# Attention and three residual blocks on one core: four background banks, single score banks, and maximum units in bursts of two

## What is computed

```
x = x + attn(layernorm(x))
    scores = K Q^T / 8;  scores[q < k] = 1e-10
    probs  = softmax(scores);  out = (probs V) W_out + bias
x = x + ffn(layernorm(x))
    w = (q / 7.5 - 1) * scale  (per group of 16);  y = x w^T + bias + (x la^T) lb^T
```

## Time and profile before

| | |
|---|---|
| three timed runs, us | 2410.23, 2406.73, 2414.44 (median 2410.23) |
| profiled execution: time, span | 2404.84, 2403.0 |
| PE busy | 2249.6 us, 94% of the span |
| VectorE, ScalarE, GpSimd busy | 1312.2, 869.7, 1341.8 us |
| mean granted clock of TensorE | 0.981 |

### The profile page before, as it was taken

How to read it: one execution, slowest core, us unless ns; L and a number is a source line. 1 busy time by engine, 2 the same in 40 slices (tenths; PEclk the granted TensorE clock), 3 DMA queues, 4 the chain that set the end, 5 groups by cost and what they waited for, 6 DMA issues and landing times. The chain is left out here.

```text
span 2403.0 us, 30679 instructions
## 1 busy us (share of the span) xinstructions
PE 2249.6 (94%) x10080; PEld 1147.3 (48%) x10080; DVE 1312.2 (55%) x3555; ACT 869.7 (36%) x1266; POOL 1341.8 (56%) x1231
## 2 busy tenths in 40 slices
PE   5999999999999998999999999999999988899987
PEld 2344444444444444444444444444444444767764
DVE  4755555555555555464646463646464663365664
ACT  3244444433434335434343434343434343011111
POOL 2176767666767676676767575757575741111110
PEclk9699999999999999999999999999999999999998
DMA  4534444443535362535353535363635431521100
GB/s 115 131 95 125 113 125 113 116 121 104 134 103 134 99 173 72 139 94 139 91 147 87 148 86 149 79 158 79 156 78 157 107 94 54 188 88 62 62 18 18
DMA packets 206268, 261.30 MB, mean 109 GB/s; under 512 B 74720, under 2 KB 91296, under 8 KB 206112
## 3 DMA queue, kind: packets, MB, share of 16 engines
q1 hardware_dynamic: 206112, 259.35, 40.9%
HBM read 169.87 MB, written 88.87 MB: 108 GB/s over the span
## 5 line engine op out<-in xcount | busy, mean ns | idle before, releaser
L689 POOL TENSOR_TENSOR acc<-acc,probs 128x512 f32<-128x512 f32 (+1 forms) x900 | 970.8, 1115 | 387.7 <-ACT probs L1039 387.7
L1039 ACT ACTIVATE probs<-ps_s 128x1024 f32<-128x1024 f32 (+2 forms) x640 | 551.9, 899 | 414.6 <-PE ps_s L836 172.8
L1094 DVE TENSOR_REDUCE partial<-ps_bg 128x1 f32<-128x512 f32 x768 | 491.1, 685 | 232.7 <-PE ps_bg L778 230.6
L834 PE MATMUL ps_s<-qq,kk 128*128 128x512 f32 (+3 forms) x1280 | 574.5, 449 | 26.8 <-ACT probs L1039 26.8
L855 PE MATMUL ps_o<-probs,v 128*64 128x512 f32 (+3 forms) x2560 | 541.2, 544 | 5.2 <-DVE num L1118 5.1
L836 PE MATMUL ps_s<-qm,kl 128*128 128x512 f32 (+3 forms) x1280 | 469.0, 366 | 0.0
L726 PE MATMUL ps_bg<-home,w_in 128*128 128x512 f32 x768 | 366.5, 601 | 14.9 <-DVE split L1076 10.8
L834 PEld LDWEIGHTS ps_s<-qq,kk 128*128 128x128 f32 x1280 | 244.6, 191 | 213.8 <-issue 155.2
L778 PE MATMUL ps_bg<-k_bf,q_bf 64*128 64x512 bf16 (+3 forms) x1280 | 272.3, 365 | 44.1 <-DVE split L1076 21.1
L1091 DVE CUSTOM_DVE_ANT_0 junk<-ps_bg,mask_q 128x512 bf16<-128x512 f32 (+3 forms) x512 | 230.8, 485 | 103.6 <-issue 102.4
L855 PEld LDWEIGHTS ps_o<-probs,v 128*64 128x64 f32 x2560 | 155.9, 136 | 236.1 <-issue 209.4
(11 more groups left out here) (109 smaller groups left out, 1889.1 us busy)
## 6 DMA issues: line engine op xcount, KB each, us to landing
high_and_low<-split SPq DMA_DIRECT2D x128, 512.0 KB, 5.9
qq<-high_and_low SPq DMA_DIRECT2D x64, 512.0 KB, 4.3
kk<-high_and_low SPq DMA_DIRECT2D x128, 256.0 KB, 5.2
qm<-high_and_low SPq DMA_DIRECT2D x64, 256.0 KB, 5.9
kl<-high_and_low SPq DMA_DIRECT2D x64, 256.0 KB, 6.3
e<-masked_weights SPq DMA_DIRECT2D x128, 128.0 KB, 3.0
scale<-inverse_sums SPq DMA_DIRECT2D x128, 128.0 KB, 2.9
heads_turned<-num SPq DMA_DIRECT2D x64, 256.0 KB, 3.5
```

Source lines behind the costliest of these rows:

```text
L689: g.tensor_tensor(acc[h][:, group % 2, q0:q0 + w], acc[h][:, group % 2, q0:q0 + w], probs[h][:, probs_slot(i, t), at:at + w], ALU.add).the ...
L834: pe.matmul(out, kk[:, h, kb * P:(kb + 1) * P], qq[:, h, q], start=True, stop=False, skip_group_check=True)
L1039: nc.scalar.activation(probs[h][:, probs_slot(i, t), 0:width], ps_s[:, h, 0:width], ACT.Exp, scale=SCORE_SCALE).then_inc(p_ready, 1)
L1094: e.reduce_max(to, of, AX.X).then_inc(max_read, 1)
```

## The change

It changes the tables and, with them, several things in each part of the attention:

- `ps_bg` gets four banks, `ps_s` three single ones. A tile is now four halves (three or two on the diagonal) of up to 512 columns, each with its own bank, its own wait of PE for the exponential three halves back, and its own exponential.
- the 40 maximum units stand in 20 bursts of two, at 20 slots.
- ACT does the exponential of a half in the slot in which PE makes its scores, and the slot's copies behind it.
- in the head, units 0 to 11 stand among projections 4 to 11; odd transposes go through `ps_s`, the second of each even one through `ps_o`.
- the layer norm of batch 1 is done in tiles, one a slot, at other slots; denominators are read in their own slot (`DEN_LAG` 0).
- a code matrix is turned into weights behind the additions of a given tile of pair 15, the last two behind another step of POOL.

```diff
-MAX_AT = [11, 15, 17, 21, 23, 27, 29, 33, 35, 37, 39, 41, 45, 47, 49, 51, 53, 57, 59, 61, 63, 65, 69, 71,
-          73, 75, 77, 81, 83, 85, 87, 89, 93, 95, 99, 101, 105, 107, 111, 113]
+BURSTS = [11, 15, 21, 27, 33, 39, 45, 51, 53, 57, 63, 69, 71, 75, 81, 87, 93, 99, 105, 111]
+MAX_AT = [BURSTS[n // 2] for n in range(NMAX)]
...
-DEN_LAG = 1
+DEN_LAG = 0
...
-BANKS = 3
-
-STATS_AT = {3: 52, 2: 58, 1: 70, 0: 82}
+BANKS = 4
+FIRST_ORDER = [("proj", 0), ("turn", 2), ("proj", 1), ("proj", 2), ("proj", 3), ("max", 0), ("max", 1), ("turn", 1),
+               ("proj", 4), ("max", 2), ("max", 3), ("proj", 5), ("proj", 6), ("max", 4), ("max", 5), ("turn", 0),
+               ("proj", 7), ("max", 6), ("max", 7), ("proj", 8), ("proj", 9), ("max", 8), ("max", 9),
+               ("proj", 10), ("max", 10), ("max", 11), ("proj", 11)] + [("max", n) for n in range(12, NMAX)]
+SCORE_BANKS = 3
+def halves_of(t):
+    tile = TILES[t][1]
+    return [[n for n in range(2) if tile[n][3] // CH == half] for half in range(2 if tile[1][3] >= CH else 1)]
...
+STATS_AT = {3: 50, 2: 56, 1: 66, 0: 78}
...
-XN_AT = {3: 70, 2: 76, 1: 88, 0: 100}
-TURN_AT = {3: 80, 2: 90, 1: 102, 0: 112}
+XN_AT = {3: 67, 2: 73, 1: 85, 0: 97}
+TURN_AT = {3: 76, 2: 82, 1: 94, 0: 106}
+CODES_TILE = [3, 4, 5, 6, 9, 10]
...
-FIRST_FIN_AT = [5, 8, 11, LAST_MAX[3] + 3, LAST_MAX[2] + 3, LAST_MAX[1] + 3, NMAX]
+FIRST_FIN_AT = [8, 14, 16, LAST_MAX[3] + 3, LAST_MAX[2] + 3, LAST_MAX[1] + 3, NMAX]
...
-        ps_s = ctx.enter_context(nc.psum_tensor("ps_s", [P, 2, 2 * CH], F32))
+        ps_s = ctx.enter_context(nc.psum_tensor("ps_s", [P, SCORE_BANKS, CH], F32))
...
                 def dequantise(l):
 
+                    pool.wait_ge(added_last, START + pool_ops_before(CODES_TILE[l] + 1))
...
-                            to = ps_s[:, n % 2, s * CH:(s + 1) * CH]
+                            to = ps_s[:, s] if n % 2 else (ps_s[:, 2], ps_o)[s]
...
-                def scores(t, h, n):
+                def scores(i, t, h, n):
...
-                    out = ps_s[:, h, at:at + w]
+                    blocks = halves_of(t)[at // CH]
+                    k = half_index(i, t, h, at // CH)
+                    if n == blocks[0] and k >= SCORE_BANKS:
+                        pe.wait_ge(p_ready, START + k - SCORE_BANKS + 1)
+                    bank_s = ps_s[:, k % SCORE_BANKS]
+                    out = bank_s[:, at % CH:at % CH + w]
...
-                                pe.wait_ge(p_ready, START + 2 * NT * i + 2 * t + h + 1)
...
+                    act.wait_ge(s_ready, START + k + 1)
+                    nc.scalar.activation(probs[h][:, probs_slot(i, t), CH * half:end],
+                                         ps_s[:, k % SCORE_BANKS, 0:end - CH * half], ACT.Exp,
+                                         scale=SCORE_SCALE).then_inc(p_ready, 1)
```

More of the change, by code:

```diff
@@ L697, in _ @@
                 normalise(N - 2, 0)
-                for l in range(n_layers):
+                for l in range(4):
                     dequantise(l)
                 masked_part(N - 1, 2)
+                for l in range(4, n_layers):
+                    dequantise(l)
                 normalise(N - 1, 3)
@@ L884, in _ @@
                 turn_x(0, 3)
[L885 to L896, removed]
+                for what, n in FIRST_ORDER:
+                    if what == "proj":
+                        project(0, n)
+                        continue
+                    if what == "turn":
+                        turn_x(0, n)
+                        continue
                     max_unit(0, n)
@@ L971, in standardise, with standardise_tile @@
                 def standardise(batch, c):
+                    for t in range(4):
+                        standardise_tile(batch, c, t)
+                def standardise_tile(batch, c, t):
                     n = ln_count(batch, c)
                     b = n % 2
[L975 to L979, removed]
+                    if t == 0:
+                        act.wait_ge(shift_done, START + n)
+                    last = nc.scalar.activation(chunk_rows[c][:, t, :], chunk_rows[c][:, t, :], ACT.Identity,
+                                                bias=shift[:, b, t:t + 1], scale=rstd[:, b, t:t + 1])
+                    if t == 3:
+                        last.then_inc(xn_done, 1)
                 def take_x(batch, c):
@@ new lines, in _ @@
+                for h in range(2):
+                    for n in range(2):
+                        exponentials(0, 0, h, n)
+                evacuate(0, "mt", 0, NFIRST)
+                for i in range(N):
+                    for n in range(SLOTS):
+                        t = n // 6 + 1
+                        if n % 6 < 4 and t < NT:
+                            exponentials(i, t, n % 6 // 2, n % 2)
+                        elif n % 6 < 4 and i + 1 < N:
+                            exponentials(i + 1, 0, n % 6 // 2, n % 2)
+                        for u in range(NPROJ):
+                            if PROJ_SLOT[u] == n and i + 1 < N:
+                                high(i + 1, u)
+                        for k, (kind, c, at) in enumerate(FIN):
+                            if at == n and kind != "den" and pair_of(i, kind, c) < N:
+                                evacuate(pair_of(i, kind, c), kind, c, fin_before(i, k) + 1)
+                        for c in PROJ_CHUNKS:
+                            if next_batch(i) is not None and XN_AT[c] <= n < XN_AT[c] + 4:
+                                standardise_tile(next_batch(i), c, n - XN_AT[c])
+                            if next_batch(i) is not None and TURN_AT[c] == n:
+                                take_x(next_batch(i), c)
```

124 lines of the change are left out of this document (67 added, 57 removed).

## The result

The changed kernel takes 2489.07 us (median of four runs, 2474.72 to 2492.87), the kernel before 2411.88 in the runs beside it. The ratio is 1.031, with a 95% interval of 1.027 to 1.036. It is slower, as forecast, but by 77 us and not by 11: the time lies far outside the range of 2380 to 2445.

The account below looks back on a forecast made before the run. PE in its program order was taken as the bound. Steady pairs -7, clock +20, head +7, layer norm -7, last pair 0 and late transfers -2 summed to +11 us, forecast 2419 us, with 2380 to 2445 for 8 in 10.

Parts of the forecast that it names:

- The burst's waits: Bursts behind projections wait for the bank's reading: 2.16 us at slots 21, 27, 0.7 at 15, 33; 5.9 a pair.
- The saving by bursts: Maximum units in twos save PE shape switches and places between score blocks: 3.2 us a pair, ends 1.0 and 3.2.
- the price of a denominator ahead of a burst: Later in the pair, a values turn or denominator just ahead of a burst adds 0.3 us twice and 0.1 twice.
- the close bursts: Bursts two slots apart (51 and 53, 69 and 71): the fourth half waits some 0.45 us each time.
- the -2 for late transfers: A fourth bank softens late transfers that cost a few pairs 1 to 2 us: -2 us in all.
- the clock: PE's clock falls behind 12 of 30 waits of 2.16 us in the pairs, 1.7 us each: +20, ends none and 51.
- The head: Maximum units among projections win nothing: +2 us at full clock, +5 for clock falls, +7 in all.
- The layer norm: Batch 1's layer norm in pieces of one tile hides better in its pair: -7 us, from -9 to -3.
- The last pair: Codes leaving DVE's additions give -1.5 us, PE stopping at the fourth block +1.8: taken as 0, from -4 to +3.
- The score banks: PE's fourth block of a tile just fits behind the exponential's reading: nothing charged, 1.5 us a pair at most.
- The clock falls in nearly every wait: Rival for the pairs: PE stops for exponentials in most tiles, or nearly every wait brings a fall; 2435 to 2460, chance 0.16.
- The bursts' waits are hidden: Rival for the pairs: the bank is read sooner than 4.18 us, -5 us a pair; about 2340 to 2390, chance 0.15.

Follow-up runs that it names:

- Experiment 1: The changed kernel with the bursts of slots 15, 21, 27 and 33 moved to 17, 23, 29 and 35, behind the weighted sums: 2385.1 us, ratio 0.991.
- experiment 9: The changed kernel with single maximum units and batch 1's layer norm in whole chunks, both at the slots of before: 2346.6 us, ratio 0.972.

## Why the prediction was wrong

**The bound** was right. PE in its own order sets the time in the pairs, and the runs differ there by PE's waits and clock.

**The burst's waits** behind projections were the right mechanism, rightly sized. From start to next start in the good pair, less the same burst without a wait: slots 21 and 27 lose 2.06 us each (2.16 forecast), slots 15 and 33 0.80 and 0.69 (0.7 each); visible are 1.68, 1.68, 0.58 and 0.31. Slot 11 was under-sized: 0.2 forecast, 1.06 lost there, and 1.0 visible on average. The saving by bursts came too: 0.54 us for four matmuls where two single units take 0.64. Experiment 1 shows the waits by their absence.

**The step that failed first was the price of a denominator ahead of a burst.** Values turns and denominators there were put at "0.3 twice and 0.1 twice"; the turns at slots 50 and 86 cost 0.26 and 0.37 us, the denominator at slot 98 0.20, but that at slot 110 far more. At slot 111 it is 2.27 us visible on average (2.58 from start to next start in the good pair), 32 us in fourteen pairs, and seven clock falls on top. I had counted bank uses but taken every reader to be ready. This reader waits for its own transfer, 2.66 us in the row above, and the change put it ahead of the maximum readings. The visible waits of a plain pair came to 7.6 us on average. That this is also the sum of the two forecasts, 5.9 and 1.7, is luck: the brackets leave out what is counted as busy, and from start to next start the bursts of the good pair lose 10.5 us, with only 0.08 and 0.33 at the close bursts of slots 53 and 71 (0.45 each forecast). Free of falls the good pair is 122.2 us where I said 119.8, and the denominator's burst alone accounts for the difference of 2.4. Over the thirteen plain pairs, waits and bare time make +19 us, where -0.5 a pair and the -2 for late transfers stood.

**The term that was mis-sized most is the clock.** I counted 30 waits and took 12 falls of 1.7 us, +20 us. There were 34 spells from 234 us to 2019 us, 126 us long, and they cost 56 us more than the two of before. I had assumed that a wait behind a dense projection is kinder to the clock; 22 of the 28 waits of 1.68 us in these pairs had a spell behind them, 7 of the denominator's, and 5 spells belong to slot 11 and the layer norm. The price of one spell, 1.6 us measured, was right. The swings that the Trainium skill describes (TensorE: Matmul & The Clock Gate, A second HAM failure mode: psum-queue depth-cycling) are in this trace, in 22 of 28 such waits; the section gives no price. With a fall in each of the 30 waits the sum was 51 us, nearer than mine. It was written down as the high end and then discounted without a row that bore on the difference. Nor was "one of the two such rows" the whole of them: the trace of before has a third wait of this size, with the clock at 1.00 behind it (PE's timeline, then the view by stretches):

```profile
1102.27 1.98 PE L726 MATMUL ps_bg<-home,w_in 128*128 128x512 f32 x4 [2.30 <-DVE split L1076]
...
1102.27:1106.00 3.73, 3.73 (x16) 2.25 (x17) 1.52 (x6) 1.71 (x4) 2.36 (x3) 1.00 0.40 124
```

One fall behind three waits said little on how many would follow thirty.

**The head** was forecast at +7 and came to +10.2. The steps up to projection 10 came within 2.6 us (forecast and measured start: projection 4 at 37.9 and 37.4, 7 at 49.7 and 50.8, 10 at 61.7 and 64.2, 11 at 66.5 and 69.3); unit 12 was read from 73.5, not 69.1, and the last unit starts 5.4 us later than before (103.34 against 97.92), inside what was forecast. What was left out is SP's queue: the gathers of the stacks start when the last projection is done, 78.1 us and not 61.3, and the maxima's way to the scores lies behind their 6 MB. From 78 to 106 us the DMA engines are 96% busy, and PE waits 4.54 us for the maxima.

**The layer norm** was forecast at -7. Its pair grew by 8.3 us, of which 8 are clock; its pieces bring little (experiment 9). **The last pair** was taken at 0 and came to -2.6. **The score banks** cost nothing, as forecast: one wait of 3.47 us for an exponential in the last pair, none in the others.

**The rivals.** "The clock falls in nearly every wait" (2435 to 2460, 0.16) was closest and still 29 us short, since the denominator's wait stood in no case. "The bursts' waits are hidden" (2340 to 2390) is what experiment 1 made of the kernel by putting 0.9 to 1.9 us of other work in between.

## What to carry to other kernels

With banks that rotate, look for the use as many places back as there are banks, and ask of its reader not only how long it reads but what it waits for itself, queue and transfers included. A burst of as many uses as there are banks makes PE wait for whatever stands just ahead of it; put other PE work between the two, or leave the uses apart. When a wait has been taken away, look at the same chain one step further before counting the gain: here moving one burst cost 26 us, and moving one reciprocal behind two readings gave 73.

## What the runs showed of the hardware

How often the clock fell behind a wait of PE, counted over the traces of all fourteen kernels in their fourteen pairs from the first denominator of chunk 0 to the fifteenth. A spell at 0.50 counts to a wait when it begins between the wait's start and 3.4 us behind its end; waits within a spell that had already begun count as without.

| visible wait, us | followed by a fall |
|---|---|
| 0.6 to 1.0 | 0 of 149 |
| 1.0 to 1.3 | 3 of 52 |
| 1.3 to 1.5 | 5 of 40 |
| 1.5 to 1.62 | 5 of 8 |
| 1.62 to 1.75 | 69 of 89 |
| 1.75 to 2.2 | 14 of 23 |
| 2.2 to 2.5 | 43 of 66 |
| 2.5 and more | 35 of 36 |

Length is not all: in the changed kernel the same 1.68 us were followed by a fall in 9 of 14 cases at slot 21 and in 13 of 14 at slot 27. Why, no run here separates. Of its 34 spells in these pairs 32 lasted 3.41 us.
